# The step orders of a pipelined int8 attention: values and query turn moved ahead of input turn and output

## The reference, cut to what matters

```
def _w8a8_linear(x, w, b):            # q and the output projection
    qx, sx = _dyn_quant(x)            # per row: max|x| / 127, then round
    qw, sw = _quant_weight(w)
    return einsum('bnc,oc->bno', qx, qw) * (sx * sw[:, 0]) + b
q = _w8a8_linear(layernorm(x), wq, bq)        # 16 heads of 32
k = cond @ wk.T + bk ; v = cond @ wv.T + bv   # 64 context rows a batch
attn = softmax(q k / sqrt(32) + mask)
x = x + tanh(g) * _w8a8_linear(attn v, wo, bo)
```

## Time and profile before

| what | value |
|---|---|
| three executions | 1982.28, 1983.78, 1983.98 us; median 1983.78 |
| the profiled execution | 1983.36 us, span 1981.6 us |
| busy in the span | PE 1847.4 us (93%), DVE 1098.1 (55%), ACT 1038.0 (52%), POOL 962.9 (49%) |
| second attention | about 1591 to 1767 us of the span |
| last feed-forward part alone | about 1767 us to the end |

### The profile page before, as it was taken

How to read it: one execution, slowest core, us unless ns; L and a number is a source line. 1 busy time by engine, 2 the same in 40 slices (tenths; PEclk the granted TensorE clock), 3 DMA queues, 4 the chain that set the end, 5 groups by cost and what they waited for, 6 DMA issues and landing times. The chain is left out here.

```text
span 1981.6 us, 27597 instructions
## 1 busy us (share of the span) xinstructions
PE 1847.4 (93%) x9759; PEld 1324.2 (67%) x9796; DVE 1098.1 (55%) x2264; ACT 1038.0 (52%) x2252; POOL 962.9 (49%) x865
## 2 busy tenths in 40 slices
PE   6999999999999999999997999989999968869998
PEld 4666666776766666766774887769999746644443
DVE  4544544445455654565444648524444567868886
ACT  3555656644544545544444321125656466757775
POOL 4544565444653445554431100007888446657774
PEclk8999999999999999999999999999999979989999
DMA  7111111211012111111010300136888870000000
GB/s 236 45 50 50 48 34 44 66 31 50 34 34 71 49 50 42 30 52 48 2 64 20 109 30 22 43 109 194 241 227 253 220 160 1 1 0 23 22 17 27
DMA packets 112952, 141.18 MB, mean 71 GB/s; under 512 B 37408, under 2 KB 68128, under 8 KB 112624
## 3 DMA queue, kind: packets, MB, share of 16 engines
q1 hardware_dynamic: 105648, 122.63, 19.7%
q0 software_dynamic: 7168, 16.78, 4.0%
HBM read 104.78 MB, written 29.36 MB: 68 GB/s over the span
## 5 line engine op out<-in xcount | busy, mean ns | idle before, releaser
L743 POOL TENSOR_TENSOR a_xcl<-xT,a_xch 128x512 fp32r<-128x512 f32 x64 | 82.4, 1288 | 322.7 <-ACT a_xch L558 322.7
L898 PE MATMUL a_A<-a_pT,a_vf 128*128 128x512 f32 (+1 forms) x448 | 237.2, 611 | 0.9 <-ACT a_pT L574 0.9
L848 PE MATMUL a_S<-a_kT,a_qT 128*128 128x288 f32 (+3 forms) x640 | 210.0, 426 | 4.8 <-ACT a_qT L586 3.1
L659 DVE TENSOR_REDUCE a_nmax<-a_S 128x1 f32<-128x192 f32 (+3 forms) x256 | 138.1, 551 | 85.1 <-PE a_S L849 83.8
L564 ACT ACTIVATE a_pr_odd<-a_S,a_nmax 128x320 f32<-128x320 f32 (+1 forms) x128 | 80.9, 633 | 156.3 <-DVE a_nmax L659 155.1
L120 PE MATMUL a_A<-a_wlo,a_xch 128*128 128x512 f32 x256 | 153.3, 599 | 6.4 <-DVE a_qT L655 6.4
L848 PEld LDWEIGHTS a_S<-a_kT,a_qT 128*128 128x128 f32 x640 | 115.1, 190 | 54.5 <-issue 28.3
L574 ACT ACTIVATE a_pT<-a_TR 128x512 f32<-128x512 f32 (+1 forms) x224 | 132.2, 590 | 34.7 <-PE a_TR L888 33.8
L564 ACT ACTIVATE a_pr_even<-a_S,a_nmax 128x192 f32<-128x192 f32 (+1 forms) x128 | 67.0, 525 | 135.0 <-DVE a_nmax L659 134.9
L1503 POOL TENSOR_TENSOR e_wlo<-expert_raw,e_whi 128x1408 fp32r<-128x1408 f32 x32 | 102.7, 3232 | 66.8 <-ACT e_whi L1673 66.8
L699 DVE TENSOR_TENSOR a_otl<-a_A,a_oth 128x512 fp32r<-128x512 f32 x64 | 44.2, 691 | 152.2 <-ACT a_oth L578 152.2
(11 more groups left out here) (389 smaller groups left out, 5133.6 us busy)
## 6 DMA issues: line engine op xcount, KB each, us to landing
a_pw<-in_L_ffn_w_dram SPq DMA_DIRECT2D x96, 256.0 KB, 2.8
expert_raw<-in_L_ffn_w_gate_dram SPq DMA_DIRECT2D x16, 704.0 KB
expert_raw<-in_L_ffn_w_up_dram SPq DMA_DIRECT2D x16, 704.0 KB
expert_raw<-in_L_ffn_w_down_dram SPq DMA_DIRECT2D x16, 512.0 KB
tern<-a_tern SPq DMA_DIRECT2D x48, 128.0 KB, 1.9
x_res<-in_x_dram SPq DMA_DIRECT2D x4, 1024.0 KB, 9.2
a_raw<-in_L_xattn_wq_dram SPq DMA_DIRECT2D x4, 1024.0 KB, 6.2
a_raw<-in_L_xattn_wo_dram SPq DMA_DIRECT2D x4, 1024.0 KB, 5.4
```

What stands on the lines that cost most here:

```text
L659: ve.tensor_reduce(nmax[:, s % 2, i:i + 1], pair(s, i), AX.X, ALU.max, negate=True).then_inc(s_max, 1)
L743: pool.tensor_tensor(xcl[:, t % 2], xT[:, :, tok(t)], xch[:, t % 2].bitcast(F32), ALU.subtract).then_inc(xlo_ready, 1)
L848: pe.matmul(bank[:, lo:hi], qT[:, t % 2, hq], kT[:, par(t), lo:hi], start=True, stop=hi < nk)
L898: last = pe.matmul(A[:, A_USE["V", t, 0][0]], vf[r, par(t), i], pT[r, i % 2], start=i == 0, stop=i == nkt - 1)
```

## The change

Only strings change. On PE, V0, K0 and V1 stand ahead of T0 and Y0. On ACT, t0 stands ahead of q0, and k0 ahead of c0 and v0. On DVE, b0 goes from the head of the slot to behind M0, and N0 from behind Y0 to behind M0 and b0. The explicit lists of slots 10 to 14 on ACT and of 13 and 14 on DVE are permuted alike; PE's lists begin at slot 15 and stay.

```diff
-    PE_ORDER = "S0 U0 P0 Q0 P1 T0 Y0 V0 K0 V1"
-    ACT_ORDER = "q0 t0 i0 t1 c0 v0 k0 e0 O0"
-    DVE_ORDER = "b0 D0 o0 M0 x0 Y0 N0 m0"
+    PE_ORDER = "S0 U0 P0 Q0 P1 V0 K0 V1 T0 Y0"
+    ACT_ORDER = "t0 q0 i0 t1 k0 c0 v0 e0 O0"
+    DVE_ORDER = "D0 o0 M0 b0 N0 x0 Y0 m0"
...
-    ACT_JOIN = {10: "q0.12 t0.9 i0.11 t1.9 c0.13 v0.13 k0.11 G0.0 e0.10 O0.9",
+    ACT_JOIN = {10: "t0.9 q0.12 i0.11 t1.9 k0.11 c0.13 v0.13 G0.0 e0.10 O0.9",
...
-                13: "q0.15 t0.12 i0.14 t1.12 fc0.0 fv0.0 k0.14 e0.13 O0.12",
-                14: "t0.13 i0.15 t1.13 fc0.1 fv0.1 k0.15 e0.14 O0.13 fq0.0 fq1.0",
+                13: "t0.12 q0.15 i0.14 t1.12 k0.14 fc0.0 fv0.0 e0.13 O0.12",
+                14: "t0.13 i0.15 t1.13 k0.15 fc0.1 fv0.1 e0.14 O0.13 fq0.0 fq1.0",
...
-    DVE_JOIN = {13: "fb0.0 D0.13 o0.11 M0.13 x0.15 Y0.11 N0.12",
-                14: "fb0.1 D0.14 o0.12 M0.14 Y0.12 N0.13 fm0.0",
+    DVE_JOIN = {13: "D0.13 o0.11 M0.13 fb0.0 N0.12 x0.15 Y0.11",
+                14: "D0.14 o0.12 M0.14 fb0.1 N0.13 Y0.12 fm0.0",
```

## The result

The changed kernel takes 1963.11 us, the median of four executions (1957.93, 1961.13, 1965.09, 1966.53), against 1983.18 of the kernel before beside it (1982.28 to 1983.98): a ratio of 0.9898, with a 95% interval of 0.9877 to 0.9919. The forecast was 1967.8 with a range of 1965 to 1976.

What follows compares the result with a forecast made beforehand. A loop of waits through PE's order was taken to set the 9.26 us slot; with DVE's list as bound, slots of 7.83, less gain lost to scalings, end 16.0 us earlier: 1967.8 us, range 1965 to 1976.

Steps and rivals of the forecast that it cites:

- The bound before: Last stage's slots: a loop of waits, with V0, K, V1 behind Y, which needs DVE's o, sets 9.26 us.
- DVE becomes the bound: New slot: DVE's list of 7.81 us exceeds ACT's loop of 7.67, with 0.14 to spare.
- The rival that ACT's loop takes over: Rival: four more hand-overs of 0.15 make ACT's loop 8.27 a slot; about 1975 us, chance 0.15.
- The longer loop: Loop through DVE, POOL's s, ACT, PE and DVE: 15.26 us over two slots, 7.63 per slot.
- DVE's list, 7.81 plus 0.02: DVE's eight start-to-start distances sum to 7.81 us a slot, plus 0.02 surplus for new neighbours: eight slots of 7.83.
- The scalings: Slots 10 to 12: an extra ACT scaling of 0.94 makes ACT's loop 8.61; three slots give back 2.17 us.
- Startup and join: Slot 1's N at about 1618.2, slot 2's 7.65 later; slots 13 and 14 to D of tile 15 take 12.0.
- What follows moves as a block: After D of tile 15 the order is unchanged and no DMA is left, so all of it moves 16.0 us earlier.
- The sum: D of tile 15 at 1726.1 instead of 1742.16; 1983.36 less 16.0 is 1967.4, plus 0.4 for the median: 1967.8.
- The port rival: Rival: b on DVE blocked by POOL's s for 1.90 us a slot; slot 9.71, total 1991, chance 0.07.
- No change: Rival: PE's wait merely shifts, or the last stage starts by something else than tile 15; 1983.8 us, chance 0.05.
- more gain: Rival: hand-overs shorter than the rows have them, or scalings covered after all; 1965.5 us, chance 0.03.

Runs made afterwards that it cites:

- e8: Kernel before with the change's DVE and ACT orders, PE's order as before: median 1985.81 us, ratio 1.0003 to 1.0027 to before.
- e7: Changed kernel with bn_stats run twice in each of b's tiles on DVE: slot 8.44 us, median 1972.14, ratio 0.9922 to 0.9966 to before.
- e6: Changed kernel with the copy x moved from DVE to ACT behind O: slot 8.22 us, median 1975.49, ratio 0.9952 to 0.9976 to before.
- e3: Kernel before with only PE's order changed: slots 9.17 and 10.72 us, median 1992.51, ratio 1.0032 to 1.0071 to before.
- e10: Changed kernel run a third time, no edit: last stage 372.6 us, median 1962.57, ratio 0.9879 to 0.9910 to before.
- e9: Changed kernel with the three scalings moved behind O on ACT, second run: last stage 370.3 us, median 1962.61, ratio 0.9864 to 0.9903 to before.

## Why the prediction was right, and where it was not

The mechanism was right, and the slot came within 0.1 us; the time fell below the range mostly because the sum took all that stands ahead of the last stage as fixed.

- *The bound before* was a loop of waits through PE's order. Right: e8 leaves that order and keeps 9.30 a slot, with T released by o.
- *DVE becomes the bound.* Right: no idling ahead of N in the plain slots, and e7's lengthening goes straight into the slot. The rival that ACT's loop takes over did not come; its distance of 0.14 agrees with the estimates from e6 and from the scalings (0.15 and 0.13). The longer loop over two slots, 7.63 a slot, was not tested by itself.
- *DVE's list, 7.81 plus 0.02.* This is the term of the slot that was too large: 7.71. The rows of before gave N as 2.02 (now 1.99, its first instruction taking 0.22 instead of 0.26), x as 0.39 (0.34), D as 1.14 (1.13), b as 0.96 (0.95), Y as 0.67 (0.66); m measures 1.18 for 1.17. N had been measured behind a wait, which may be why, though without one it still takes 0.25 in e3. x's 0.39 held a Y that overlapped x by 0.02 only, where it is 0.08 now; Y had probably still waited for PE's product, which the trace of before has until 1672.03, just ahead of Y at 1672.07. The surplus of 0.02 came as forecast (7.73 against 7.71). Eight slots: 62.6 forecast, 61.8 measured.
- *The scalings.* Right in place, cause and size: they add 2.11 to three slots of 7.71, where 2.17 was forecast. The three slots took 25.24 for 25.66 forecast, because the slot itself was shorter. In ACT's loop v takes 0.19 from start to start, not 0.25, and e 0.95, not 0.97.
- *Startup and join.* From the stage's start to the first N 27.7 were forecast (1618.2 less 1590.5); it was 27.43, 26.88 and 26.84 in the three profiles of the changed kernel. With 27.94 and 26.24 in the two of the kernel before, no gain or loss of the change can be read from that. To slot 2's N 7.57 (7.65 forecast), from slot 13's N to D of tile 15 11.94 (12.0).
- *What follows moves as a block.* Right in sum: from D of tile 15 to the end 239.6, 239.3 and 239.2, against 239.4 before, and the span.
- *The sum.* e10 shows it best, since it begins like the profiled execution of before: D of tile 15 at 1723.92 where 1726.1 was forecast, 18.2 us earlier than in the earlier trace rows instead of 16.0. Of the missing 2.2 us, 0.9 are startup (no more than the scatter just named), 0.8 the eight slots, 0.4 the three slots with scalings and 0.1 the two pieces of 0.08 and 0.06. By stage times, which hold that scatter too, the gain is 17.4 (390.4 to 373.0, means of two and three profiles). e10's execution took 1964.86 us.
- *The step that failed* is the last one of the sum: "The profiled execution took 1983.36 ... less 16.0", with 0.4 for the median and nothing for how far executions differ. It holds all that stands ahead of the last stage fixed, on three runs 1.7 us apart, and the runs showed in its place that executions of that same code spread over 9 us and that the changed kernel began its last stage at 1582.5, 1583.6 and 1590.5. The prediction itself gave 4 us as what this kernel's timing can tell, and put the lower end of its range 2.8 under the forecast. The four executions of the changed kernel fell into different bunches (1957.93, 1961.13, 1965.09, 1966.53), while those of before all lie at 1982.28 to 1983.98; so the medians are 20.1 us apart where the stage times are 17.4. So a lower end of 1965 was too high. Of the 4.7 us between forecast and median, 1.4 are the last stage (17.4 for 16.0), above all its slot of 7.83 that measured 7.73; 0.6 are the kernel before, whose median was 1983.18 beside the changed one and not 1983.78; the other 2.7 are left for the bunches (an estimate, by subtraction). Even with e10's late start the changed kernel took 0.14 less than the range allows, so the size of the gain alone would have missed it in that execution, by little.
- *The port rival* fell: b takes 0.68 and N's product 0.69, both beside POOL's s. The Trainium skill, "SBUF — State Buffer", § Who interferes with whom, exempts a DVE instruction with at most one SBUF input outside the two-port modes; N's product reads PSUM and one SBUF operand, and the trace agrees.
- *No change, and more gain.* No change is excluded by the ratio. "More gain" named the right direction (shorter hand-overs) at 0.03, which was too little: of the eight terms of DVE's list five came out smaller than their rows had them, two equal and one larger.

## What to carry to other kernels

When engines run fixed lists, add up each list from start to start and each loop of waits; the largest is the slot, and an edit can gain only down to the next largest, here from 9.26 to DVE's list of 7.71, with ACT's loop an estimated 0.13 to 0.15 below that. Reordering one engine's list may only move the wait to another (PE's order alone was slower, DVE's and ACT's without PE's no faster), so lists that feed one another are best looked at, and changed, together. Idle time is room only for steps whose readers can wait: the same gap took a scaling for nothing and cost 0.5 us a slot when it got a step that U needed. And before a single span is subtracted from another, see whether the stages that weren't touched took as long.

## What the runs showed of the hardware that wasn't expected

- Behind a wait of PE of 1.98 us the granted clock fell in some slots and not in others of the same shape, and where it fell the slot cost 1.55 us more (10.72 against 9.17, e3).
- One program on one core runs in bunches of executions some 8 us apart (1954.48 and 1954.75, then 1962.61 to 1963.65 for e9), and over the twelve profiles the granted clock between 50 and 75 us (0.86, 0.94, 1.00) goes along with when the last stage begins. Drops of the granted clock that only one of two executions has stand where their common instructions move apart (1.4, 1.8, 1.5 and 1.7 us at the drops near 44, 68, 590 and 1576 us, the kernel before against the changed one).
